# A language model's fused layers: the dense tiles take three PSUM score banks in the order 0, 1, 2, 1

## The chip, the cores and the metric

The kernel runs on one core of a Trainium2 chip. Its time is the device time in microseconds (us); three runs of the kernel before gave 3267.7, 3269.15 and 3270.88 us, and the median is 3269.15 us. The core has five engines that run side by side, each in the order of its own instructions: PE (TensorE, matrix products), ACT (ScalarE), DVE (VectorE), POOL (GpSimd) and SP (which issues transfers). They wait for each other through semaphores. PSUM is the memory that PE writes to; it has eight banks of 128 x 512 f32, and this kernel uses all eight.

## The reference

The reference is a small language model of two layers on 4 sequences of 1024 tokens with 64 channels. The part that matters here is the feed-forward block of the first layer: product keys choose 16 of 4096 values for each token and head, and the values are mixed by a softmax.

```
q = (x @ Wq_pk).reshape(b, n, P, HEADS, DIM_KEY)            # two halves of a query
sim = einsum('pbnhd,pkhd->pbnhk', q, pk_keys)               # 64 scores for each half
scores, idx = top_k(sim, 16)
score = scores[0][..., :, None] + scores[1][..., None, :]   # sums of a row's and a column's score
final_scores, pk_idx = top_k(score, 16)
final_scores = softmax(final_scores)
k = einsum('bnhk,bnhkd->bnhd', final_scores, keys_table[ind])
v = einsum('bnhk,bnhkd->bnhd', final_scores, values_table[ind])
```

The keys and values so found go through causal attention with 8 heads, after that come a plain attention and a mixture of 8 experts. There are 16 (sequence, head of 0 to 3) pairs, and each pair carries a second head (4 to 7) with it.

## The kernel before, in words

A first part (embedding, a convolution by Fourier matrices, a gate) ends in this profile at 353 us. The stage `mixer_stage` follows, and what is said from here on is all in it. It has 22 time slots of 64 positions each (`SLOT = 64`). Every engine has its own loop over all positions `q`, and does at each position what the tables (`area_uses`, `extra_uses`, `STEPS_AT`) put there. So the order on each engine is written out in advance, and the same position of different engines belongs together only through semaphores.

One head of a pair finds its values by gathers of table rows: POOL issues them (L1402), ACT scales the rows (L1691), DVE sums them once in eight positions (L2013). The other head does without gathers, by a dense product over all 4096 values. This dense product is what the change touches. For a pair it has 64 tiles: two halves of 512 tokens, 32 tiles each (`TILES`), each tile 128 values by 512 tokens. In the dense loop `c` numbers the tiles over all pairs, 1024 in all. A tile goes through four steps:

- `score_dense(c)` on PE: the 128 x 512 scores into a PSUM bank `D_ps` (L1417, L1420). The score of a value is a sum of a row's and a column's part. A *corner* is the set of tiles that share the same two operands `U[.., 2 + jh, ..]` and `U[.., ih, ..]`. Within a corner there are eight tiles (`eighth` 0 to 7), and the scores of the next differ from those of the one before by one product. So the bank keeps the scores of the last tile, and one product of 96 x 128 by 96 x 512 in bf16 (L1420) adds the difference. Only where a bank begins a corner, or is taken over in its midst, is a product with `start=True` made first (L1417), and the tile is called *fresh*.
- `exp_dense(c)` on ACT (L1623): the exponential of the bank into `W`, a ring of six buffers in SBUF.
- `mask_dense(c)` on DVE (L1787): reads the bank again and sets to zero in `W` what lies below the threshold. It raises the semaphore `w_done`.
- `apply_dense(c)` on PE (L1430): the product of the table's tile with `W`, summed into `acc`. In the profile it is two instructions, as every f32 product here.

At position `q`, with `c = q - 64`, PE does in this order: the scores of tile `c + 3`, `apply_dense(c)`, the weighting of the attention (`weigh`, L1442), the attention's scores into two other banks called `area` (L1456, L1476, L1486 and more), and one further small task through the bank `X` (L1523 to L1581). ACT does at the same position the exponential of tile `c + 3` and then the rest of its work, DVE its maxima of `area` first, its other work, and the mask of tile `c + 3` among or behind it.

Before the change tile `c` uses bank `c % 3`. Its scores may be written when the mask of tile `c - 3` is done (`pe.wait_ge(w_done, c - 2)`). Since `apply_dense(c)` waits for the mask of tile `c` anyway, that wait and the wait of the scores of tile `c + 3` are for the same mask.

Tiles are named in what follows by their number within the pair, 0 to 63; the first half is 0 to 31, the second 32 to 63. Tile `t` is scored at position `t - 3`. In the order before, the corners of a half are begun at its tiles 0, 1, 2 (one in each bank), and the fourth corner is shared by the three banks at tiles 24, 25, 26 of the half: six fresh tiles in a half.

## Time and profile before

| what | value |
|---|---|
| median of three runs | 3269.15 us |
| span of the profiled execution | 3918.3 us |
| PE busy | 3008.9 us, 77% |
| DVE busy | 2785.8 us, 71% |
| POOL busy | 2057.7 us, 53% |
| ACT busy | 2039.4 us, 52% |
| scores of the dense tiles, L1420 and L1417 | 1024 and 192 matmuls |
| masks of the dense tiles, L1787 | 1024, 683 ns each |

The profiled execution has no time of its own beside its span, so the span stands for it. It is 649.2 us longer than the median of the runs. The busy time of an engine is the union of its instructions; a matmul's end is modelled, and the spacing of the starts of two matmuls that follow each other is shorter than the duration shown.

### The profile page before, as it was taken

The page shows a single profiled execution, that of the slowest core. Times are in us where ns is not written, and L with a number is a line of the kernel's source. Part 1 is how long each engine was busy: PE and PEld are TensorE (multiplying, and loading weights), DVE is VectorE, ACT ScalarE, POOL GpSimd, SP SyncE. Part 2 cuts the span into 40 slices and gives each one's busy share as a digit, 9 for nine tenths or more (in the row PEclk, how much of TensorE's full clock was granted, in tenths as well). Part 3 has the DMA queues.
Part 4 walks back from the last instruction along what each step waited for, and adds up shares of the span by engine and source line. Part 5 has one row for each costly group of instructions (what it writes and reads, how often), then busy time and mean ns, then how long its engine had stood idle before and what let it go on. Part 6 is the DMA issues. An engine that isn't in the chain of part 4 may idle for free.

```text
span 3918.3 us, 39268 instructions
## 1 busy us (share of the span) xinstructions
PE 3008.9 (77%) x9722; PEld 1391.1 (36%) x9722; DVE 2785.8 (71%) x9999; ACT 2039.4 (52%) x4498; POOL 2057.7 (53%) x2095
## 2 busy tenths in 40 slices
PE   4861657878787878878778868888778878888888
PEld 2430223333333333333333433333333433333343
DVE  7678777777777777776777887777768786874433
ACT  3231545555555555655555655556555655555532
POOL 3011666666656665555565655556656655655400
PEclk8985777888787888989888989888888988989899
DMA  1001121212121111112121212111111212121100
GB/s 37 22 8 52 44 66 43 62 45 57 48 56 47 52 52 50 52 46 55 44 59 38 65 40 57 44 52 53 51 50 46 57 46 56 42 62 39 33 3 3
DMA packets 85626, 179.86 MB, mean 46 GB/s; under 512 B 40177, under 2 KB 41107, under 8 KB 85398
## 3 DMA queue, kind: packets, MB, share of 16 engines
q0 software_dynamic: 66560, 135.40, 13.1%
q1 hardware_dynamic: 18838, 41.94, 3.5%
q8 instruction: 79, 1.29, 0.1%
q14 instruction: 149, 1.22, 0.1%
HBM read 176.15 MB, written 1.05 MB: 45 GB/s over the span
## 4 chain that ended last, share of the span: by engine, by line
PE 41%; DVE 25%; another core or an unknown queue 11%; issue 8%; ACT 8%; ACTq 0%; DVEq 0%
PE mx_acc L1430 12%; PE mx_O L1442 7%; PE mx_area L1476 6%; DVE mx_W L1787 5%; PE mx_D L1420 4%; ACT mx_GT L1691 3%; DVE mx_KVs L2013 3%; PE mx_area L1456 2%; ACT mx_W L1623 2%; DVE mx_mx_part L2031 2%; PE mx_area L1492 1%; DVE mx_mx L2031 1%; PE mx_X L1560 1%; PE mx_area L1486 1%
## 5 line engine op out<-in xcount | busy, mean ns | idle before, releaser
L1402 POOL DMA_INDIRECT mx_G<-in_kv_table,mx_slot_i x2048 | 2004.0, 978 | 1394.6 <-issue 590.1
L1430 PE MATMUL mx_acc<-mx_W,mx_table 128*128 128x512 f32 x2048 | 1180.7, 660 | 1.6 <-ACT mx_kvT L1630 0.7
L1787 DVE SCALAR_TENSOR_TENSOR mx_W<-mx_D,mx_W 128x512 f32<-128x512 f32 x1024 | 699.1, 683 | 297.5 <-ACT mx_W L1623 180.5
L1623 ACT ACTIVATE mx_W<-mx_D 128x512 f32<-128x512 f32 x1024 | 606.6, 593 | 523.2 <-PE mx_D L1420 231.0
L1691 ACT ACTIVATE mx_GT<-mx_G,mx_slot_w 128x128 f32<-128x128 f32 x2048 | 759.2, 495 | 3.2 <-DVE mx_KVs L2013 1.1
L1420 PE MATMUL mx_D<-mx_U,mx_pick_b 96*128 96x512 bf16 x1024 | 432.7, 423 | 110.8 <-DVE mx_W L1787 52.5
L1430 PEld LDWEIGHTS mx_acc<-mx_W,mx_table 128*128 128x128 f32 x2048 | 436.1, 214 | 201.9 <-issue 104.5
L1647 ACT ACTIVATE mx_PT<-mx_area 128x512 f32<-128x512 f32 x472 | 241.8, 514 | 464.9 <-PE mx_area L1480 146.3
L1442 PE MATMUL mx_O<-mx_PT,mx_KVs 128*65 128x512 f32 (+3 forms) x768 | 347.5, 536 | 170.0 <-ACT mx_PT L1647 82.8
L1456 PE MATMUL mx_area<-mx_KTa,mx_QTa 64*128 64x512 f32 (+3 forms) x384 | 200.6, 607 | 132.6 <-DVE mx_mx L2031 66.1
L2013 DVE TENSOR_REDUCE mx_KVs<-mx_GT 128x128 f32<-128x2048 f32 x128 | 291.9, 2280 | 6.0 <-ACT mx_GT L1691 5.9
L1442 PEld LDWEIGHTS mx_O<-mx_PT,mx_KVs 128*65 128x65 f32 x768 | 105.4, 146 | 388.3 <-issue 277.5
L1476 PE MATMUL mx_area<-mx_QTa,mx_KTa 65*128 65x512 f32 (+3 forms) x384 | 187.9, 574 | 70.5 <-DVE mx_mx_part L2031 61.3
L1420 PEld LDWEIGHTS mx_D<-mx_U,mx_pick_b 96*128 96x128 bf16 x1024 | 110.2, 108 | 355.7 <-issue 173.2
L1476 PE MATMUL mx_area<-mx_QTb,mx_KTb 128*128 128x512 f32 (+3 forms) x384 | 175.9, 542 | 44.4 <-DVE mx_mx_part L2031 25.6
L1456 PE MATMUL mx_area<-mx_KTb,mx_QTb 64*128 64x512 f32 (+3 forms) x384 | 202.8, 612 | 0.0
L2031 DVE TENSOR_REDUCE mx_mx_part<-mx_area 128x2 f32<-128x1024 f32 (+3 forms) x128 | 130.7, 1021 | 90.5 <-remote 43.0
L2054 DVE RECIPROCAL mx_rz<-mx_X 128x4 f32<-128x4 f32 x72 | 13.0, 180 | 247.1 <-remote 135.2
L1456 PEld LDWEIGHTS mx_area<-mx_KTa,mx_QTa 64*128 64x128 f32 x384 | 64.4, 210 | 291.0 <-issue 172.2
L1476 PEld LDWEIGHTS mx_area<-mx_QTa,mx_KTa 65*128 65x128 f32 x384 | 77.9, 211 | 175.6 <-issue 85.1
L1476 PEld LDWEIGHTS mx_area<-mx_QTb,mx_KTb 128*128 128x128 f32 x384 | 78.1, 209 | 138.9 <-issue 88.7
L1535 PE MATMUL mx_X<-mx_ident_b,mx_PC 128*96 128x128 bf16 x512 | 51.8, 260 | 95.3 <-remote 46.0
(390 smaller groups left out, 4462.4 us busy)
## 6 DMA issues: line engine op xcount, KB each, us to landing
mx_table<-in_kv_dense SPq DMA_DIRECT2D x64, 512.0 KB
mx_G<-in_kv_table,mx_slot_i POOLq DMA_INDIRECT x2048
tz_table<-in_c_dft SPq DMA_DIRECT2D x1, 2048.0 KB
tz_table<-in_c_idft SPq DMA_DIRECT2D x8, 256.0 KB, 2.6
out_h<-mx_xc SPq DMA_DIRECT2D x4, 256.0 KB
mx_G<-in_c_pick SPq DMA_DIRECT2D x1, 528.0 KB
st_h<-in_tok_W,em_ids POOLq DMA_INDIRECT x32
st_keys<-in_pk_keys SPq DMA_DIRECT2D x1, 512.0 KB, 3.9
```

The source lines that it names most:

```text
L1402: pool.indirect_dma_start(G[g % RING][:, r, :], None, a["kv_table"], bass.IndirectOffsetOnAxis(slot_i[n % 2][:, k, r:r + 1], 0))\
L1420: pe.matmul(D_ps[c % 3][:, :], pick_b[:, step, :], U[n % 2][:, ih, cols], start=False, stop=True, skip_group_check=True).then_inc(d_ready, 1)
L1430: pe.matmul(acc[:, :], table[:, tile, :], W[c % TILE_RING][:, :], start=(tile == 0), stop=(tile == TILES - 1)).then_inc(applied, 1)
L1442: pe.matmul(O_ps[0:D + 1, first:HALF], values, PT[k % 4][:, first:HALF], start=(kb == 0), stop=last, skip_group_check=True).then_inc(weigh ...
L1456: last = pe.matmul(area[x][:, 0:w], QT[x][lanes[x], qb * P:qb * P + P], KT[x][lanes[x], kh * HALF:kh * HALF + w], start=True, stop=not dia ...
L1476: last = pe.matmul(bank[:, first:HALF], KT[x][:, kb * P:kb * P + P], QT[x][:, group * HALF + first:(group + 1) * HALF], start=True, stop=n ...
L1623: act.activation(W[c % TILE_RING][:, :], D_ps[c % 3][:, :], ACT.Exp).then_inc(p_done, 1)
L1647: act.activation(PT[k % 4][:, first:HALF], area[cnt.bank[use]][:, first:HALF], ACT.Gelu if use[0] == "HID" else ACT.Exp).then_inc(prob_rea ...
L1691: last = act.activation(GT[:, :, i], G[g % RING][:, i, :], ACT.Copy, scale=slot_w[n % 2][:, k, i:i + 1])
L1787: dve.scalar_tensor_tensor(W[c % TILE_RING][:, :], D_ps[c % 3][:, :], 0.0, W[c % TILE_RING][:, :], ALU.is_ge, ALU.mult).then_inc(w_done, 1)
L2013: dve.tensor_reduce(both, rows, AX, ALU.add).then_inc(kv_ready, 1)
L2031: dve.tensor_reduce(dst, banks[:, :, 0:w], AX, ALU.max).then_inc(scores_taken, 2)
```

## The change

Tiles take the banks in the order 0, 1, 2, 1 (`BANK_OF`, by `c % 4`). Odd tiles all use bank 1, even tiles banks 0 and 2 in turn. A half has 16 odd tiles in bank 1, which are two corners of eight, and 8 tiles each in banks 0 and 2, which are one corner each. So the corners begin at the tiles 0, 1, 2 and 17 of a half, and nowhere else: four fresh tiles and not six. `corner_of` says which corner and eighth a tile is; the table of values is laid out by the same function, outside the kernel, so its tiles come in the new order by themselves. The wait before the scores follows the bank: an even tile waits for the mask of tile `c - 4`, an odd one for the mask of tile `c - 2`.

```
 RING = 2
 TILE_RING = 6
+BANK_OF = (0, 1, 2, 1)
...
 def corner_of(tile):
-    bank, step = tile % 3, tile // 3
-    pair, eighth = (bank, step) if step < 8 else (3, 3 * bank + step - 8)
-    return pair // 2, pair % 2, eighth, step in (0, 8)
+    if tile % 2:
+        pair, eighth = 2 + tile // 16, tile // 2 % 8
+    else:
+        pair, eighth = tile // 2 % 2, tile // 4
+    return pair // 2, pair % 2, eighth, eighth == 0
...
+        def D_of(c):
+            return D_ps[BANK_OF[c % 4]][:, :]
...
                 if c >= 3:
-                    pe.wait_ge(w_done, c - 2)
+                    pe.wait_ge(w_done, c - 1 if c % 2 else c - 3)
                 if fresh:
-                    pe.matmul(D_ps[c % 3][:, :], pick_b[:, 0, :], U[n % 2][:, 2 + jh, cols], start=True, stop=False,
+                    pe.matmul(D_of(c), pick_b[:, 0, :], U[n % 2][:, 2 + jh, cols], start=True, stop=False,
                               skip_group_check=True)
-                step = 1 + eighth // 3 if fresh else 3 + eighth
-                pe.matmul(D_ps[c % 3][:, :], pick_b[:, step, :], U[n % 2][:, ih, cols],
+                step = 1 if fresh else 3 + eighth
+                pe.matmul(D_of(c), pick_b[:, step, :], U[n % 2][:, ih, cols],
                           start=False, stop=True, skip_group_check=True).then_inc(d_ready, 1)
...
-                act.activation(W[c % TILE_RING][:, :], D_ps[c % 3][:, :], ACT.Exp).then_inc(p_done, 1)
+                act.activation(W[c % TILE_RING][:, :], D_of(c), ACT.Exp).then_inc(p_done, 1)
...
-                dve.scalar_tensor_tensor(W[c % TILE_RING][:, :], D_ps[c % 3][:, :], 0.0, W[c % TILE_RING][:, :],
+                dve.scalar_tensor_tensor(W[c % TILE_RING][:, :], D_of(c), 0.0, W[c % TILE_RING][:, :],
                                          ALU.is_ge, ALU.mult).then_inc(w_done, 1)
```

The change touches the order of PE alone; ACT, DVE, POOL and SP keep every instruction in its place. `mx_D0` to `mx_D2` are the three banks, `mx_W0` to `mx_W5` the ring, `mx_U0` the operand of the first pair; the lines of the changed kernel are numbered six higher, L1423 for L1417, L1426 for L1420, L1436 for L1430. The first place is PE in the second half of the first pair, at the scores of tiles 56, 57 and 58, before:

```order
L1417 MATMUL mx_D2<-mx_U0,mx_pick_b 128x512 [waits mx_w_done]
L1420 MATMUL mx_D2<-mx_U0,mx_pick_b 128x512
L1430 MATMUL mx_acc<-mx_W5,mx_table 128x512 [waits mx_w_done]
L1417 MATMUL mx_D0<-mx_U0,mx_pick_b 128x512 [waits mx_w_done]
L1420 MATMUL mx_D0<-mx_U0,mx_pick_b 128x512
L1430 MATMUL mx_acc<-mx_W0,mx_table 128x512 [waits mx_w_done]
L1417 MATMUL mx_D1<-mx_U0,mx_pick_b 128x512 [waits mx_w_done]
L1420 MATMUL mx_D1<-mx_U0,mx_pick_b 128x512
L1430 MATMUL mx_acc<-mx_W1,mx_table 128x512 [waits mx_w_done]
```

The same three tiles on PE now:

```order
L1426 MATMUL mx_D0<-mx_U0,mx_pick_b 128x512 [waits mx_w_done]
L1436 MATMUL mx_acc<-mx_W5,mx_table 128x512 [waits mx_w_done]
L1426 MATMUL mx_D1<-mx_U0,mx_pick_b 128x512 [waits mx_w_done]
L1436 MATMUL mx_acc<-mx_W0,mx_table 128x512 [waits mx_w_done]
L1426 MATMUL mx_D2<-mx_U0,mx_pick_b 128x512 [waits mx_w_done]
L1436 MATMUL mx_acc<-mx_W1,mx_table 128x512 [waits mx_w_done]
```

Three matmuls are gone here, and the banks stand in another order. The second place is PE in the same half at the scores of tiles 48, 49 and 50, before:

```order
L1420 MATMUL mx_D0<-mx_U0,mx_pick_b 128x512 [waits mx_w_done]
L1430 MATMUL mx_acc<-mx_W3,mx_table 128x512 [waits mx_w_done]
L1420 MATMUL mx_D1<-mx_U0,mx_pick_b 128x512 [waits mx_w_done]
L1430 MATMUL mx_acc<-mx_W4,mx_table 128x512 [waits mx_w_done]
L1420 MATMUL mx_D2<-mx_U0,mx_pick_b 128x512 [waits mx_w_done]
L1430 MATMUL mx_acc<-mx_W5,mx_table 128x512 [waits mx_w_done]
```

Tiles 47 to 50 on PE now, the first two rows being tile 47 and what follows it:

```order
L1426 MATMUL mx_D1<-mx_U0,mx_pick_b 128x512 [waits mx_w_done]
L1436 MATMUL mx_acc<-mx_W2,mx_table 128x512 [waits mx_w_done]
L1426 MATMUL mx_D0<-mx_U0,mx_pick_b 128x512 [waits mx_w_done]
L1436 MATMUL mx_acc<-mx_W3,mx_table 128x512 [waits mx_w_done]
L1423 MATMUL mx_D1<-mx_U0,mx_pick_b 128x512 [waits mx_w_done]
L1426 MATMUL mx_D1<-mx_U0,mx_pick_b 128x512
L1436 MATMUL mx_acc<-mx_W4,mx_table 128x512 [waits mx_w_done]
L1426 MATMUL mx_D2<-mx_U0,mx_pick_b 128x512 [waits mx_w_done]
L1436 MATMUL mx_acc<-mx_W5,mx_table 128x512 [waits mx_w_done]
```

Tile 49 is tile 17 of the second half and is fresh now, so one matmul is added; it goes to bank `mx_D1`, which tile 47 used two tiles earlier.

## Rows read from the trace of the kernel before

**Rows 1.** The profile's page: span, then busy time and share of each engine.

```profile
span 3918.3 us, 39268 instructions
PE 3008.9 (77%) x9722; PEld 1391.1 (36%) x9722; DVE 2785.8 (71%) x9999; ACT 2039.4 (52%) x4498; POOL 2057.7 (53%) x2095
```

**Rows 2.** The page's chain of waits, share of the span by engine.

```profile
PE 41%; DVE 25%; another core or an unknown queue 11%; issue 8%; ACT 8%; ACTq 0%; DVEq 0%
```

**Rows 3.** Busy time by stretch: us, PE, PEld, DVE, ACT, POOL busy (count), PEclk, DMA.

```profile
353.00:3711.00 3358.00, 2628.79 (x8360) 1189.00 (x8361) 2448.72 (x9099) 1871.63 (x4196) 2000.40 (x2045) 0.86 0.18 50
...
1551.00:1560.00 9.00, 9.00 (x21) 3.90 (x22) 5.85 (x35) 5.33 (x13) 6.54 (x7) 0.64 0.33 97
1560.00:1576.00 16.00, 16.00 (x53) 7.52 (x52) 12.96 (x72) 8.90 (x22) 11.00 (x13) 1.00 0.18 48
```

**Rows 4.** Instructions on mx_D: ns min/median/max, first and last start.

```profile
L1417 PE MATMUL mx_D<-mx_U,mx_pick_b x192: 379/381/634, 353.4 to 3690.9; 96*128 96x512 bf16 x192
```

**Rows 5.** The chain of waits in order of time, second halves: start, us, what.

```profile
747.36 0.22 PE mx_D L1417
...
1570.46 0.22 PE mx_D L1417
1570.68 0.22 PE mx_D L1420
...
3691.04 0.22 PE mx_D L1417
```

**Rows 6.** The chain of waits by line, 1645 to 1652 us, first half of pair 6.

```profile
by line: DVE mx_V L1814 29.8%; DVE mx_mxl_part L2042 25.6%; issue 24.0%; DVE mx_W L1787 17.0%; DVE mx_S L1808 11.1%; DVE mx_I L1807 5.5%
```

**Rows 7.** Timeline, tiles 13 to 15 of pair 6: start, us, instruction, idle before it.

```profile
1646.14 0.38 PE L1420 MATMUL mx_D<-mx_U,mx_pick_b 96*128 96x512 bf16 x1
...
1646.20 0.68 DVE L1787 SCALAR_TENSOR_TENSOR mx_W<-mx_D,mx_W 128x512 f32<-128x512 f32 x1
...
1646.56 0.60 ACT L1623 ACTIVATE mx_W<-mx_D 128x512 f32<-128x512 f32 x1 [0.70 <-issue]
...
1649.62 2.07 PE L1486 MATMUL mx_area<-mx_KTl,mx_QTl 128*128 128x512 f32 x2 [2.24 <-remote]
...
1652.70 0.67 DVE L1787 SCALAR_TENSOR_TENSOR mx_W<-mx_D,mx_W 128x512 f32<-128x512 f32 x1
```

**Rows 8.** Timeline, mask of tile 43 and scores of tile 45, pair 5.

```profile
1533.50 0.68 DVE L1787 SCALAR_TENSOR_TENSOR mx_W<-mx_D,mx_W 128x512 f32<-128x512 f32 x1
...
1534.18 0.38 PE L1420 MATMUL mx_D<-mx_U,mx_pick_b 96*128 96x512 bf16 x1
```

**Rows 9.** Timeline, masks of tiles 46 and 47 and scores of tile 49, pair 5.

```profile
1539.95 0.67 DVE L1787 SCALAR_TENSOR_TENSOR mx_W<-mx_D,mx_W 128x512 f32<-128x512 f32 x1
...
1542.20 1.02 PE L1476 MATMUL mx_area<-mx_QTa,mx_KTa 65*128 65x512 f32 x2
...
1544.09 0.39 PE L1420 MATMUL mx_D<-mx_U,mx_pick_b 96*128 96x512 bf16 x1 [0.87 <-remote]
...
1548.37 0.18 DVE L2054 RECIPROCAL mx_rz<-mx_X 128x4 f32<-128x4 f32 x1 [7.75 <-remote]
...
1550.23 0.68 DVE L1787 SCALAR_TENSOR_TENSOR mx_W<-mx_D,mx_W 128x512 f32<-128x512 f32 x1
```

**Rows 10.** Timeline, a mask and the scores that waited for it.

```profile
490.65 0.68 DVE L1787 SCALAR_TENSOR_TENSOR mx_W<-mx_D,mx_W 128x512 f32<-128x512 f32 x1
...
491.39 0.39 PE L1420 MATMUL mx_D<-mx_U,mx_pick_b 96*128 96x512 bf16 x1 [0.91 <-DVE mx_W L1787]
```

**Rows 11.** Timeline, first and last odd tile scored ahead of the mask two tiles back.

```profile
401.01 0.39 PE L1420 MATMUL mx_D<-mx_U,mx_pick_b 96*128 96x512 bf16 x1 [0.29 <-DVE mx_W L1787]
401.89 0.67 DVE L1787 SCALAR_TENSOR_TENSOR mx_W<-mx_D,mx_W 128x512 f32<-128x512 f32 x1
...
3692.11 0.69 DVE L1787 SCALAR_TENSOR_TENSOR mx_W<-mx_D,mx_W 128x512 f32<-128x512 f32 x1 [3.43 <-issue]
3692.39 0.38 PE L1420 MATMUL mx_D<-mx_U,mx_pick_b 96*128 96x512 bf16 x1
```

## The prediction

> **What bounds the kernel now.** I read the page first. PE is busy 77% of the span and DVE 71% [rows 1], and the chain that ended last gives PE 41%, DVE 25%, and 11% to something the profile can't name [rows 2]. So neither engine alone sets the time. The busy time by stretch says the same: in the mixer, from 353 to 3711 us, PE is busy 2628.8 of 3358 us and DVE 2448.7 [rows 3]. Only a look at where in a pair each of them leads helps.
>
> The chain in order of time, laid against the tile numbers, gives a clear pattern. In the second half of a pair it runs along PE: from 1560 to 1576 us PE is busy all 16 us at a granted clock of 1.00 [rows 3], and the products for fresh tiles stand one behind the other in the chain, 0.22 us each [rows 5]. In the first half, from about tile 15 to 38, it runs along DVE: between 1645 and 1652 us every named line of it is DVE's [rows 6]. This matters, since the change takes matmuls from PE and tightens PE's wait for DVE.
>
> The profiled span is 3918.3 us [rows 1], 649.2 us above the median of 3269.15 us. Much of that is stalls of the profiled execution: at 1540 us DVE stands 7.75 us until something the profile can't name [rows 9], and the same gap comes back at the same tile of most pairs. I take them as absent from the timed runs, an assumption the traces can't prove. The sum is therefore a difference in us of durations at full clock, made on the profiled execution and carried over to the median unscaled.
>
> **The change part by part.** *Matmuls removed.* 32 halves had six fresh tiles, 192 in all [rows 4]; now they have four. Removed are 32 x 3 = 96 products at tiles 24 to 26 of a half, added are 32 at its tile 17: 64 fewer. The duration shown is 381 ns [rows 4], but a matmul that follows another starts 0.22 us after it [rows 5], and this is what one costs PE. All 64 are 64 x 0.22 = 14.1 us of PE's time.
>
> The Trainium skill, Perfetto Trace Analysis, section "Tensor Engine Instruction (MATMUL, LD_WEIGHTS)", says that the profiler estimates a matmul's end from its size and does not observe it. By the duration the 64 would be worth 24.4 us, by the spacing 14.1 us; the trace sides with the spacing.
>
> What of them lies on the path? In the chain of waits I counted the products of the old fresh tiles. Of the 48 in second halves (tiles 56 to 58) 38 are on it, the first at 747.36 and the last at 3691.04 us [rows 5]; of the 48 in first halves (tiles 24 to 26) 4. Removing them gives 42 x 0.22 = 9.2 us. The added ones: in the second half tile 49 lies in the stretch that PE leads, so all 16 count, 16 x 0.22 = 3.5 us. In the first half tile 17 lies where the chain passes to DVE; I take 8 of 16, 1.8 us. Net gain: 9.2 - 3.5 - 1.8 = 3.9 us. The ends are 0 and 14.1 us.
>
> *The wait of odd tiles.* It was for the mask three tiles back, it is now for the mask two back. Behind it on PE, in order, stand the apply of tile c - 3, the attention's weighting and scores, and the small task in bank X; ACT waits for all of them. In the trace of before, 157 of the 508 odd tiles from the ninth on were scored before the mask two back had ended, the first by 1.55 us (401.89 + 0.67 - 401.01) and the last by 0.41 us [rows 11]. Over all of them this is 296 us of PE held back. This is the largest number of the case, and nearly all of it should cost nothing:
>
> It happens where DVE is behind, and there PE's work isn't wanted yet. Tile 15 of pair 6 was scored at 1646.14, while the mask of tile 13 ended at 1646.88 us; it would be held 0.74 us and 0.06 for the semaphore. But PE stands 2.24 us at the next scores for L1486 anyway, which need DVE too, and the mask of tile 15 starts only at 1652.70, 5.5 us after the exponential's end at 1647.16 [rows 7]. The delay is gone before anybody misses it. Where the attention's scores are consumed by DVE, at positions 16 to 38 and the early ones of the plain attention, PE can't run two positions ahead in any case.
>
> What is left are the second halves, which PE leads. The mask of tile 43 ends at 1534.18, and tile 45 is scored at 1534.18 us [rows 8]. It would be held by the semaphore alone; a matmul that waited started 0.06 us after the mask's end (490.65 + 0.68 to 491.39) [rows 10]. 16 x 0.06 = 1.0 us. Tile 49 was scored at 1544.09, after an idle time that the stall made; PE was free at 1542.20 + 0.86 = 1543.06 (two f32 matmuls, by their spacing). The mask of tile 47 needs, from DVE's reciprocal to its own end, 1550.91 - 1548.37 = 2.54 us, and could have begun at 1540.62, so it would end at 1543.16 [rows 9]. Hold: 0.10 + 0.06 = 0.16 us, in 16 pairs 2.6 us. Tile 59 looks worse in the profile, but its exponential had been held by a stall too. So the wait costs 3.6 us. The ends: 0, if PE soon stands for the attention's output anyway and that swallows it, and 296 us, which would need every hold to reach the end; the row nearest to the second halves is tile 49's, and I stay with it.
>
> *The wait of even tiles.* It is for the mask four back, so the scores no longer stand for the mask that the apply behind them needs. After such a wait PE has 0.22 us less to do. Where PE waits for a mask DVE leads, so I take 0; the other end is 16 such places on PE's stretches, -3.5 us.
>
> *The bank itself.* Exponential and mask keep their form and their order, and each bank still has one writer and two readers in turn. 0. The first part and the last 207 us of the span contain none of these lines: 0.
>
> **Sum.** -3.9 + 3.6 + 0 = -0.3 us. Predicted: 3269.15 - 0.3 = 3269 us, no change within what a measurement can tell. A difference of 0.2% (6.5 us) is about what a measurement of this kernel can tell from none.
>
> **Rivals.** *Faster: the second halves take the whole gain.* PE is busy 16 of 16 us there [rows 3], and all three of the removed products are on the chain. If the holds at tiles 45 and 49 vanish in PE's idle time behind them, if the 16 added at tile 49 lie beside a wait as well, and if even tiles give back their 3.5 us, the gain is 9.2 + 3.5 = 12.7 us: 3256 us. For it: the three stand in a stretch without one gap. Against it: part of that stretch is the backlog of the stall before it, which the timed runs don't have, and then DVE, with 12.96 of 16 us busy, may lead there now and then. Chance 0.29.
>
> *Slower: the odd tile's wait costs a position of lead behind each heavy mask.* DVE's sum over the gathered rows stands ahead of the masks of tiles 3, 11, 19 and so on, which are all odd, so it is always the tile two later, odd too, that stands for it. PE then comes to its work of that position late, and with a stock of two positions instead of three DVE runs dry when its light positions follow. It decides from the point at which DVE, once past the heavy mask, is quicker through a position than PE. Price: without tiles 49 and 59 the holds sum to 187 us; the part of them at tiles 1 to 15 and 39 to 63, outside the positions where DVE's maxima hold PE anyway, is 73 us. If a third of that reaches the end it is 24 us, and with the 3.6 us above and without 3.9 gained it is 3269.15 + 28 = 3297 us; a sixth gives 3285. Against it: PE at these places was ahead by as much as it would be held. Chance 0.24 for everything above 3276 by this way.
>
> *Slower: the clock.* After the stall that ends at 1548 us [rows 9] its granted clock is 0.64 on average for 9 us, where it is 1.00 afterwards [rows 3]: the lower level of 1.2 GHz for the larger part of it. If longer stands brought one more such fall in each pair, PE would lose 0.36 x 9 = 3.2 us each time, 52 us in all: 3321 us. The holds found are below 2 us nearly everywhere, so I give it 0.04.
>
> The Trainium skill, TensorE: Matmul & The Clock Gate, section "A second HAM failure mode: psum-queue depth-cycling", says that short idles between groups of matmuls while cycling through PSUM banks can make the clock swing. Here the banks cycle before and after alike. It would be the case just named; by the page alone it could be likely, by the rows it is not.
>
> *The change does less than it says.* The order of PE shows 64 matmuls fewer, so this is excluded.
>
> **How the numbers follow.** No change 0.43 (3263 to 3276 us), faster 0.29, slower by the lost lead 0.24, slower by the clock 0.04. That makes faster by over 0.2% 0.29, within 0.2% 0.43, slower 0.28. The range leaves out a little of each end: from 3254, the whole gain, to 3290, where a fifth of the 73 us and a little more would reach the end. The likeliest case alone is 3263 to 3276 us.
>
> **What would show it.** In the changed kernel's profile L1423 must stand 128 times. If the sum is right, the waits of PE for masks move from even to odd tiles and grow in total, while DVE's idle time ahead of its masks stays. If the faster rival holds, the chain in second halves has lost the three products and gained nothing at tiles 45 and 49. If the slower one holds, DVE idles more before the masks of tiles 4 to 8 and 46 to 50, behind ACT, which waits for PE. The prediction is wrong if the median is outside 3263 to 3276 us, and its sum is wrong, even with the median right, if DVE's idle time ahead of its masks moves by more than a third.

## The result, and the profile after

The change made the kernel a little slower. Seven runs of the changed kernel have a median of 3280.16 us (3275.51 to 3285.37), seven runs of the kernel before beside them 3270.88 us (3266.13 to 3274.51). The ratio is 1.0027, with a 95% interval of 1.0014 to 1.0040. The prediction was 3269 us and no change; the measured 0.27% is small, but its interval leaves out zero. The median lies outside the 3263 to 3276 us that the prediction had named for its likeliest case. Three executions in the whole case took far longer (4128.66, 7041.87 and 15431.88 us), and the ratios leave them out.

The page of the changed kernel, span, busy time and chain of waits, answers to [rows 1, 2]:

```profile
span 3273.6 us, 39140 instructions
PE 2786.8 (85%) x9658; PEld 1315.2 (40%) x9658; DVE 2749.4 (84%) x9999; ACT 2021.9 (62%) x4498; POOL 2061.7 (63%) x2095
...
PE 39%; DVE 28%; POOL 10%; issue 7%; ACT 5%; DMA 2%; POOLq 0%; ACTq 0%; DVEq 0%
```

Two things are new. The span is 645 us shorter than the 3918.3 us of [rows 1], and lies where the timed runs lie. And POOL, which no step of the prediction spoke of, has a tenth of the chain. Neither is the change's doing. The kernel before, profiled once more as the run `e0_before`, gives nearly the same page:

```profile
span 3274.6 us, 39268 instructions
PE 2793.2 (85%) x9722; PEld 1324.8 (40%) x9722; DVE 2748.5 (84%) x9999; ACT 2018.2 (62%) x4498; POOL 2058.3 (63%) x2095
...
PE 39%; DVE 30%; POOL 9%; issue 6%; ACT 5%; DMA 2%; ACTq 0%; DVEq 0%; POOLq 0%
...
L1402 POOL DMA_INDIRECT mx_G<-in_kv_table,mx_slot_i x2048 | 2002.3, 978 | 776.3 <-issue 605.1
...
L1691 ACT ACTIVATE mx_GT<-mx_G,mx_slot_w 128x128 f32<-128x128 f32 x2048 | 759.4, 494 | 218.9 <-DMA mx_G<-in_kv_table,mx_slot_i 217.5
L1787 DVE SCALAR_TENSOR_TENSOR mx_W<-mx_D,mx_W 128x512 f32<-128x512 f32 x1024 | 696.8, 681 | 208.4 <-ACT mx_W L1623 205.9
L1623 ACT ACTIVATE mx_W<-mx_D 128x512 f32<-128x512 f32 x1024 | 605.3, 592 | 191.7 <-PE mx_D L1420 188.6
...
L1420 PE MATMUL mx_D<-mx_U,mx_pick_b 96*128 96x512 bf16 x1024 | 407.7, 398 | 56.8 <-DVE mx_W L1787 56.1
```

So the "unknown" 11% of [rows 2] and the stalls of [rows 9] belonged to that one profiled execution. The comparisons below are made against `e0_before`. The same groups of the changed kernel, by the columns instructions | busy us, mean ns | idle us of the engine just before them, and what ended it:

```profile
L1408 POOL DMA_INDIRECT mx_G<-in_kv_table,mx_slot_i x2048 | 2003.3, 978 | 779.0 <-issue 608.2
...
L1793 DVE SCALAR_TENSOR_TENSOR mx_W<-mx_D,mx_W 128x512 f32<-128x512 f32 x1024 | 699.5, 683 | 208.9 <-ACT mx_W L1629 206.7
L1629 ACT ACTIVATE mx_W<-mx_D 128x512 f32<-128x512 f32 x1024 | 605.4, 592 | 252.1 <-PE mx_D L1426 249.0
L1426 PE MATMUL mx_D<-mx_U,mx_pick_b 96*128 96x512 bf16 x1024 | 410.1, 400 | 154.0 <-DVE mx_W L1793 153.1
```

PE now stands 154.0 us ahead of the scores, nearly all of it for masks, where it stood 56.8. That is 97 us more; ACT's idle time ahead of the exponentials grows by 60 (191.7 to 252.1). In the sum of DVE's idle time ahead of the masks almost nothing arrives (208.4 to 208.9). The last number is what the prediction had asked for, and it holds, while the timed runs are 9 us slower. The two profiled executions differ by 1 us only; that of `e0_before` was the slowest of its kernel's 12 runs (3276.48 us against a median of 3266.01). One execution scatters by as much as is sought here, so a sum over one profile can't decide a question of 0.3%; only what stands tile by tile, and the same in several kernels, can.

The products are as announced, one line of the changed kernel's instructions on L1423:

```profile
L1423 PE MATMUL mx_D<-mx_U,mx_pick_b x128: 378/381/634, 338.9 to 3030.8; 96*128 96x512 bf16 x128
```

### The profile page after: what moved, and what is told of

It reads as the page before. It is cut to its first block, busy times and chain, and to the rows that moved or that the text cites. A ratio compares the mean times of both kernels' runs of the same rounds, so it can differ in the third digit from the quotient of the medians.

```text
span 3273.6 us, 39140 instructions
## 1 busy us (share of the span) xinstructions
PE 2786.8 (85%) x9658; PEld 1315.2 (40%) x9658; DVE 2749.4 (84%) x9999; ACT 2021.9 (62%) x4498; POOL 2061.7 (63%) x2095
## 3 DMA queue, kind: packets, MB, share of 16 engines
q8 instruction: 78, 1.28, 0.2%
## 4 chain that ended last, share of the span: by engine, by line
PE 39%; DVE 28%; POOL 10%; issue 7%; ACT 5%; DMA 2%; POOLq 0%; ACTq 0%; DVEq 0%
PE mx_acc L1436 12%; POOL mx_G L1408 10%; PE mx_O L1448 6%; DVE mx_W L1793 6%; PE mx_area L1482 6%; PE mx_D L1426 3%; DVE mx_KVs L2019 3%; DMA mx_G<-in_kv_table,mx_slot_i 2%; DVE mx_mx_part L2037 2%; PE mx_area L1462 2%; ACT mx_GT L1697 2%; PE mx_area L1498 2%; PE mx_X L1566 1%; ACT mx_W L1629 1%; DVE mx_mx L2037 1%
## 5 line engine op out<-in xcount | busy, mean ns | idle before, releaser
L1436 PE MATMUL mx_acc<-mx_W,mx_table 128*128 128x512 f32 x2048 | 1108.0, 623 | 0.0
L1793 DVE SCALAR_TENSOR_TENSOR mx_W<-mx_D,mx_W 128x512 f32<-128x512 f32 x1024 | 699.5, 683 | 208.9 <-ACT mx_W L1629 206.7
L1629 ACT ACTIVATE mx_W<-mx_D 128x512 f32<-128x512 f32 x1024 | 605.4, 592 | 252.1 <-PE mx_D L1426 249.0
L1426 PE MATMUL mx_D<-mx_U,mx_pick_b 96*128 96x512 bf16 x1024 | 410.1, 400 | 154.0 <-DVE mx_W L1793 153.1
L1436 PEld LDWEIGHTS mx_acc<-mx_W,mx_table 128*128 128x128 f32 x2048 | 410.3, 202 | 164.1 <-issue 99.4
L1448 PE MATMUL mx_O<-mx_PT,mx_KVs 128*65 128x512 f32 (+3 forms) x768 | 311.9, 488 | 14.7 <-ACT mx_PT L1653 13.8
L1426 PEld LDWEIGHTS mx_D<-mx_U,mx_pick_b 96*128 96x128 bf16 x1024 | 106.0, 103 | 393.4 <-DVE mx_W L1793 271.2
L1482 PE MATMUL mx_area<-mx_QTa,mx_KTa 65*128 65x512 f32 (+3 forms) x384 | 171.5, 529 | 58.2 <-DVE mx_mx_part L2037 58.2
L1462 PE MATMUL mx_area<-mx_KTb,mx_QTb 64*128 64x512 f32 (+3 forms) x384 | 195.3, 592 | 0.0
L1482 PE MATMUL mx_area<-mx_QTb,mx_KTb 128*128 128x512 f32 (+3 forms) x384 | 157.6, 492 | 9.3 <-DVE mx_mx_part L2037 9.3
L1533 PE MATMUL mx_X<-st_keys,mx_qpk 128*128 128x256 f32 x256 | 77.3, 429 | 52.7 <-ACT mx_S L1665 32.4
L1710 ACT ACTIVATE mx_hot<-mx_FI 128x864 uint16<-128x864 uint32 x128 | 116.4, 911 | 3.6 <-DVE mx_row L1972 3.6
```

The source lines that it names most:

```text
L1426: pe.matmul(D_of(c), pick_b[:, step, :], U[n % 2][:, ih, cols], start=False, stop=True, skip_group_check=True).then_inc(d_ready, 1)
L1436: pe.matmul(acc[:, :], table[:, tile, :], W[c % TILE_RING][:, :], start=(tile == 0), stop=(tile == TILES - 1)).then_inc(applied, 1)
L1448: pe.matmul(O_ps[0:D + 1, first:HALF], values, PT[k % 4][:, first:HALF], start=(kb == 0), stop=last, skip_group_check=True).then_inc(weigh ...
L1462: last = pe.matmul(area[x][:, 0:w], QT[x][lanes[x], qb * P:qb * P + P], KT[x][lanes[x], kh * HALF:kh * HALF + w], start=True, stop=not dia ...
L1482: last = pe.matmul(bank[:, first:HALF], KT[x][:, kb * P:kb * P + P], QT[x][:, group * HALF + first:(group + 1) * HALF], start=True, stop=n ...
L1629: act.activation(W[c % TILE_RING][:, :], D_of(c), ACT.Exp).then_inc(p_done, 1)
```

## The experiments

Every kernel was timed in five rounds against the kernel before; the ratio stands with its 95% interval. Pairs are counted from 0. "Period" is the time from the end of one tile's mask to the end of the next, and sums of periods are over the pairs 1 to 15.

### The change in two: its wait and its products

`e0_before` is the kernel before, unchanged, for a second profile and as a measure of what no change looks like.

> The kernel before, unchanged, for a profile of its own beside the others. The profiled execution shown ahead of the prediction stood 649 us above its timed runs; both theories expect that this one comes out near 3272 us with a span of about the same, as the changed kernel's did (3273.6 us), and that it shows where ACT and DVE really stand. Time 3271 us.

Measured: 0.9992 (0.9980 to 1.0003), 3266.01 us.

`e1_wait_alone` is the kernel before with the odd tiles' wait of the change:

```
-                    pe.wait_ge(w_done, c - 2)
+                    pe.wait_ge(w_done, c - 1 if c % 2 else c - 2)
```

> Banks, corners and products of the kernel before; only the wait of odd tiles is tightened, from the mask three tiles back to the mask two back. Theory A (the lost lead of the odd tiles makes the change slow, and hides a gain of some 4 us of the removed products): slower than before by 9 to 14 us, about 3283 us. Theory B (the wait costs nothing, and the loss comes from the other parts, the earlier scores of even tiles or the new banks): within 3 us of before, 3271 us.

Measured: 1.0024 (1.0011 to 1.0037), 3276.1 us. The wait alone is, within the intervals, the whole slowdown.

`e2_products_alone` is the kernel before with the change's number and places of fresh products; its banks are the old ones, so the scores after tile 16 of a half are other than the reference's:

```
-    return pair // 2, pair % 2, eighth, step in (0, 8)
+    return pair // 2, pair % 2, eighth, tile in (0, 1, 2, 17)
```

> Banks and waits of the kernel before; the products that begin a bank stand at tiles 0, 1, 2 and 17 of a half, as in the change, and no longer at 24, 25, 26. The scores after tile 16 of a half are wrong by this, the work is the changed kernel's. Theory A: 4 us faster than before (3267), at most 14. Theory B: no change or up to 4 us faster as well; it is the difference of this run and the changed kernel that they must both explain.

Measured: 1.0003 (0.9992 to 1.0014), 3268.3 us. By the interval the 64 products fewer are worth between 2.6 us of gain and 4.6 us of loss. The two parts, 1.0024 and 1.0003, make up the 1.0027 of the change.

`e3_other_parity` lets the even tiles take the short wait. The heavy masks, those behind DVE's sum over gathered rows, are of tiles 3, 11, 19 and so on; an even tile never waits directly for one of them.

```
-BANK_OF = (0, 1, 2, 1)
+BANK_OF = (1, 0, 1, 2)
...
-    if tile % 2:
+    if tile % 2 == 0:
...
-                if c >= 3:
-                    pe.wait_ge(w_done, c - 1 if c % 2 else c - 3)
+                if c >= 4 or c == 2:
+                    pe.wait_ge(w_done, c - 3 if c % 2 else c - 1)
```

> The changed kernel with the parts of even and odd swapped: even tiles all use bank 1, odd tiles banks 0 and 2. The long sum of gathered rows on DVE stands ahead of odd tiles' masks, so the tile held by the mask two back is no longer the one that follows a heavy mask. Fresh tiles are 0, 1, 3 and 16 of a half. Theory A, in its form that the heavy mask is what holds: most of the loss is gone, 3265 to 3270 us. If any wait two back costs the same, whatever the parity: as the changed kernel, 3280 us. Theory B: 3280 us too, or unlike both.

Measured: 1.0035 (1.0024 to 1.0046), 3279.67 us. My theory that it takes a heavy mask fell: without one in the short wait it is no better. A lead of two tiles costs as much at the even tiles as at the odd ones.

### Banks, even tiles, and where the wait costs

`e4_banks_six_products` is the changed kernel with six products in a half, so that only banks and waits differ from before; without a fresh product at tile 17 and with those at the tiles 24 to 26 the scores from tile 17 on are other than the reference's.

```
-    return pair // 2, pair % 2, eighth, eighth == 0
+    return pair // 2, pair % 2, eighth, tile in (0, 1, 2, 24, 25, 26)
```

> The changed kernel's banks and waits, but with the beginning products at tiles 0, 1, 2, 24, 25 and 26 of a half as before, 192 in all (the scores of tiles 17 on are wrong by this, the work is that of six products). Theory A, as the first four runs leave it (the odd tiles' wait is the loss of some 8 us, the products are worth nothing): 3276 to 3280 us, as the changed kernel. If the products had been worth 4 us beside the new waits: 3284.

Measured: 1.0031 (1.0019 to 1.0043), 3277.19 us: as the change itself. `e5_even_as_before` takes from the change the looser wait of its even tiles:

```
-                    pe.wait_ge(w_done, c - 1 if c % 2 else c - 3)
+                    pe.wait_ge(w_done, c - 1 if c % 2 else c - 2)
```

> The changed kernel, with the wait of even tiles for the mask three tiles back, as before, in place of four back. Theory A: no difference to the changed kernel (3276 to 3280), since an even tile's apply waits for that mask anyway. Theory C (the earlier scores of even tiles disturb ACT's order and cost): faster than the changed kernel by 2 us or more.

Measured: 1.0022 (1.0013 to 1.0031), 3275.88 us. The looser wait of the even tiles brings nothing, as predicted.

`e6_wait_tiles_11_to_31` and `e11_wait_other_tiles` (this one ran in the next group) divide the short wait by place: odd tiles 11 to 31 of a pair, and all other odd tiles.

```
-                    pe.wait_ge(w_done, c - 2)
+                    pe.wait_ge(w_done, c - 1 if c % 2 and 11 <= c % SLOT < 32 else c - 2)
```

> The kernel before with the odd wait tightened at tiles 11 to 31 of a pair only, the place where the profile shows nearly all of PE's added idle time (0.4 to 1.2 us a tile) and DVE's added idle time ahead of the masks of tiles 14 and 15 (0.32 us a pair together). If the loss arises there: 5 to 8 us slower than before, as the tightening everywhere. If it arises at tile 5 and in the second half: within 2 us of before.

> The kernel before with the odd wait tightened at the tiles 0 to 10 and 32 to 63 of a pair, that is everywhere but at 11 to 31. With the run of tiles 11 to 31 (3276 us by its ratio of 1.002) it divides the loss of 8 us. If the loss is made at tiles 14 and 15, as DVE's added idle time there says: within 2 us of before. If tile 5 and the second half carry a part, as I first reckoned: 3 to 4 us slower.

Measured: 1.0020 (1.0007 to 1.0032) for the tiles 11 to 31, 1.0011 (1.0001 to 1.0022) for the others. By these values eleven of 32 odd tiles carry about two thirds, and they lie in the stretch in which I had judged the wait free; the two intervals overlap over most of their length, so the share itself is not shown, only that each part costs something.

`e7_apply_first` is the changed kernel with PE's apply of a position ahead of the odd tile's scores. If the loss came from the apply and the attention that stand behind a held matmul, this would have given it back.

```
-                if 0 <= c + 3 < PAIRS * SLOT:
+                if 0 <= c + 3 < PAIRS * SLOT and not (c % 2 == 0 and c >= 0 and c % TILES):
...
+                    if c % 2 == 0 and c + 3 < PAIRS * SLOT:
+                        score_dense(c + 3)
```

> The changed kernel, with the scores of an odd tile put behind apply_dense of the same position and not ahead of it (not at the first tile of a half). While PE waits for the mask two back it then has the apply, 0.86 us, to do. Theory A (the wait blocks what stands behind it): 3 to 8 us faster than the changed kernel, about 3272. If what counts is that the scores themselves come late, ACT and DVE behind them: slower than the changed kernel, 3285 or more.

Measured: 1.0065 (1.0050 to 1.0080), 3289.72 us. The theory fell, and in a useful way: the order that frees the apply and makes the scores still later costs more. It is the scores that are wanted, by ACT: against the changed kernel PE stands less ahead of the scores (154.0 to 86.1 us), but ACT's idle time ahead of the exponentials grows from 252.1 to 354.1 us and DVE's ahead of the masks from 208.9 to 259.0.

### The gathers as a floor

POOL's part of the chain asked for a test of its own. In the kernel before 2048 gathers are issued from 332.7 to 3057.4 us, 1.33 us apart on average. Where nothing holds them they are mostly 1.25 us apart, 0.94 busy and 0.30 that the profile names "issue"; the second of these two lines is one of the longer ones:

```profile
1000.00 0.94 POOL L1402 DMA_INDIRECT mx_G<-in_kv_table,mx_slot_i  x1 [0.30 <-issue]
1001.24 1.19 POOL L1402 DMA_INDIRECT mx_G<-in_kv_table,mx_slot_i  x1 [0.30 <-issue]
```

That is 128 x 1.25 = 160 us in a pair. From the last mask of one pair to that of the next it takes 162 to 171 us in eleven pairs and 177 to 180 in the other four. In the profile shown of before nobody could see it: the stalls gave POOL time to run ahead, and ACT hardly ever stood for a gather. The two groups of that page:

```profile
L1402 POOL DMA_INDIRECT mx_G<-in_kv_table,mx_slot_i x2048 | 2004.0, 978 | 1394.6 <-issue 590.1
...
L1691 ACT ACTIVATE mx_GT<-mx_G,mx_slot_w 128x128 f32<-128x128 f32 x2048 | 759.2, 495 | 3.2 <-DVE mx_KVs L2013 1.1
```

ACT's idle time ahead of the scaling is 3.2 us here and 218.9 us in `e0_before`. `e8_fifteen_rows` leaves out the gather of the sixteenth row from the third group on; the old content of the buffer is used in its place.

```
-                for r in range(TOPK):
+                for r in range(TOPK if g < RING else TOPK - 1):
...
-                    act.wait_ge(gathered[g % RING], 16 * TOPK * (g // RING + 1))
+                    act.wait_ge(gathered[g % RING], 16 * (TOPK + (TOPK - 1) * (g // RING)))
```

> The kernel before, with POOL issuing the gathers of 15 table rows and not 16 for every group after the first two (the sixteenth row of a group keeps an old value; 126 gathers left out). Theory D (POOL's row of gathers, 2048 issues 1.25 us apart, is a floor under the mixer: 2560 of the 2724 us from its first to its last): much faster, by 60 to 150 us, until DVE or PE holds. If POOL is only one of several and off the path: within 15 us of before.

Measured: 0.9789 (0.9775 to 0.9802), 3197.8 us. One gather in sixteen gone takes 70 us off, and ACT's idle time ahead of the scaling falls to 80.6 us. The floor is real. On this ground, where the other engines set the pace more often, the two parts were tried again: `e9_fifteen_rows_products` with the products of `e2_products_alone`, `e10_fifteen_rows_wait` with the wait of `e1_wait_alone`.

> As the last, with the beginning products at tiles 0, 1, 2, 17 of a half too (64 fewer). Theory D: the 64 products, worth nothing while the gathers set the pace, are worth 4 to 10 us here against the fifteen rows alone. If the gathers have nothing to do with it: within 2 us of the fifteen rows alone.

> As the fifteen rows alone, with the odd tiles' wait tightened to the mask two back. If the wait delays the chain PE, ACT, DVE itself: 8 us or more slower than the fifteen rows alone. If it only works through the gathers, which wait for masks and for ACT's scaling: within 3 us.

Measured: 0.9797 (0.9784 to 0.9811), 3201.22 us, for the products, which is no gain and so neither of the two expectations; 0.9814 (0.9801 to 0.9827), 3207.75 us, for the wait, 10 us slower than `e8_fifteen_rows`, and the runs of the two don't overlap (3197.44 to 3203.52 against 3206.63 to 3208.92). So the wait's cost isn't bound to the gathers: it is as large where their floor is loosened.

`e12_rows_three_fresh` takes away all three products at tiles 24 to 26 of a half and adds none, 96 fewer; the scores from tile 24 on are other than the reference's.

```
-    return pair // 2, pair % 2, eighth, step in (0, 8)
+    return pair // 2, pair % 2, eighth, tile in (0, 1, 2)
```

> Fifteen rows as before, and the beginning products at tiles 0, 1, 2 of a half only: 96 fewer, none added at tile 17. The profiles of fifteen rows with and without the change of products give, as means over 15 pairs, 0.40 us a pair less between the masks of tiles 55 and 60 and 0.18 us more at the mask of tile 50, behind the product added at tile 49. If both are real: 3.5 us less for the removed and added ones together, which two timed runs didn't show, and 6.4 us less here than fifteen rows alone, 3191 to 3194 us. If the removed ones are hidden after all: 3197 to 3200 us.

Measured: 0.9810 (0.9794 to 0.9825), 3204.24 us, where a real gain would have given some 3192. Its expectation was missed.

`e13_rows_wait_13_15` is `e8_fifteen_rows` with the short wait at two tiles of a pair alone:

```
-                    pe.wait_ge(w_done, c - 2)
+                    pe.wait_ge(w_done, c - 1 if c % SLOT in (13, 15) else c - 2)
```

> Fifteen rows as before, and the odd wait tightened at the tiles 13 and 15 of a pair only, 32 of 1024 tiles. The profile of fifteen rows with all odd waits tightened has 0.15 us a pair more at the mask of tile 15 and 0.30 us more at tile 17. If these two waits are the main part of the loss of 10 us: 5 to 8 us slower than fifteen rows alone, 3203 to 3206. If it is spread over all odd tiles: within 2 us of it.

Measured: 0.9815 (0.9801 to 0.9828), 3206.14 us. By the medians these 32 waits of 512 carry 8 of the 10 us. The comparison is a loose one: the two kernels were not timed in the same group, and `e12_rows_three_fresh`, which was timed beside this one and has no short wait, came out at 3204.24 us, 2 us below it. What can be compared tile by tile is firmer, and this is the run in which the mechanism can be read. First the timeline of pair 3 in `e8_fifteen_rows`: scores of 13, mask of 11, scores, exponential of 15, mask of 13, exponential and mask of 17 (start, us, instruction, idle before it and its releaser):

```profile
857.76 0.38 PE L1420 MATMUL mx_D<-mx_U,mx_pick_b 96*128 96x512 bf16 x1
857.96 0.68 DVE L1787 SCALAR_TENSOR_TENSOR mx_W<-mx_D,mx_W 128x512 f32<-128x512 f32 x1
...
860.93 0.39 PE L1420 MATMUL mx_D<-mx_U,mx_pick_b 96*128 96x512 bf16 x1 [0.85 <-DVE mx_W L1787]
861.36 0.60 ACT L1623 ACTIVATE mx_W<-mx_D 128x512 f32<-128x512 f32 x1 [0.20 <-PE mx_D L1420]
...
861.95 0.68 DVE L1787 SCALAR_TENSOR_TENSOR mx_W<-mx_D,mx_W 128x512 f32<-128x512 f32 x1
...
866.62 0.60 ACT L1623 ACTIVATE mx_W<-mx_D 128x512 f32<-128x512 f32 x1
...
867.92 0.67 DVE L1787 SCALAR_TENSOR_TENSOR mx_W<-mx_D,mx_W 128x512 f32<-128x512 f32 x1
```

The same pair in `e13_rows_wait_13_15`: mask of 11, scores of 13, mask of 13, scores and exponential of 15, exponential and mask of 17:

```profile
853.94 0.68 DVE L1787 SCALAR_TENSOR_TENSOR mx_W<-mx_D,mx_W 128x512 f32<-128x512 f32 x1
854.68 0.39 PE L1420 MATMUL mx_D<-mx_U,mx_pick_b 96*128 96x512 bf16 x1 [0.93 <-DVE mx_W L1787]
...
857.93 0.68 DVE L1787 SCALAR_TENSOR_TENSOR mx_W<-mx_D,mx_W 128x512 f32<-128x512 f32 x1
858.67 0.39 PE L1420 MATMUL mx_D<-mx_U,mx_pick_b 96*128 96x512 bf16 x1 [1.66 <-DVE mx_W L1787]
859.10 0.60 ACT L1623 ACTIVATE mx_W<-mx_D 128x512 f32<-128x512 f32 x1 [1.01 <-PE mx_D L1420]
...
864.35 0.60 ACT L1623 ACTIVATE mx_W<-mx_D 128x512 f32<-128x512 f32 x1
...
864.98 0.69 DVE L1787 SCALAR_TENSOR_TENSOR mx_W<-mx_D,mx_W 128x512 f32<-128x512 f32 x1 [1.00 <-ACT mx_W L1623]
```

Count from the start of mask 13. Its end holds the scores of 15, so they come at +0.74 where they came at -1.02. The exponential of 15 comes at +1.17 where it came at -0.59. From there to the exponential of 17 ACT has 5.25 us of work without a gap in both (exponentials, scaling, two copies of keys for each position), so that one comes at +6.42 where it came at +4.67. Mask 17 had started 0.70 us after that exponential's end, which is all that DVE had in hand; now it stands 1.00 us, and mask 17 starts at +7.05, before at +5.97. Of the 1.76 us nearly 0.7 are absorbed and 1.08 paid, not where the hold is but two tiles later. In pairs 2, 3, 4 and 5 the period of tile 17 is longer by 1.1 us each, in pairs 9 and 13 that of tile 15 by 1.0 each, 6.4 us together; `e10_fifteen_rows_wait` has the same to 0.2 us, and tile 5 of pairs 9 and 13 longer by 1.0 each besides. The other ten pairs show nothing at these tiles.

Two limits belong to this reading. The loss at tile 17 exists on fifteen rows only: with all sixteen, in `e0_before`, the mask of tile 17 already stands 1.15 us in pair 3, and its period is 2.62 us there and 2.63 in the changed kernel. And in pairs 9 and 13 of this run the granted clock fell to 0.66 for 5 us behind the held scores of tile 13, so these two are not the hold alone; the part on the clock comes back to this.

### The pace of the gathers

POOL's gathers are throttled by a wait for a mask some positions back. `e14_before_pace_10` lets them run four positions further ahead in the kernel before, `e15_after_pace_10` does the same in the changed one:

```
-                    ahead = SLOT * n + 8 * k - 6 + r // 2
+                    ahead = SLOT * n + 8 * k - 10 + r // 2
```

> The kernel before, with POOL's wait for masks loosened by four tiles (its gathers may run up to 10 tiles ahead and not 6). POOL waits 92 us for masks in the profile of before. Theory D (the gathers are the floor, and each wait of POOL before a light stretch comes back as a late gather): 10 to 60 us faster. If its waits for masks only stand in for waits for ACT's scaling, which frees the ring of two: no change.

> The changed kernel with the same loosened pace of POOL. Theory A alone: as much slower than the kernel before with the same pace as now, 8 us. With the gathers no longer the floor the removed products may show and bring it to 4 us.

Measured: 0.9979 (0.9969 to 0.9988), 3261.18 us, for the kernel before, and 1.0013 (1.0004 to 1.0022), 3271.49 us, for the changed one. The first beats both kernels of this case, by 5 us by the medians and 7 by the ratio, less than the 10 to 60 expected. The change costs 10.3 us on this ground too, not 4. POOL's wait for masks goes down from 92.3 us in `e0_before` to 38.4 us, this line of the waits of `e14_before_pace_10`, while its wait for ACT's scaling goes up from 26.0 to 61.5 us:

```profile
POOL mx_G L1402 <- DVE mx_W L1787: 38.4, 115, 3.6
```

### What a product is worth on each side

The last two runs ask why products that stood on the chain brought nothing. The kernel before repeats each of the three fresh products at tiles 24 to 26 of a half, so that it is made four times: in the second halves in `e16_products_second_half`, in the first in `e17_products_first_half` (`half == 0`). It is 144 matmuls more each, 31.7 us of PE.

```
-                if fresh:
+                for _ in range(4 if fresh and tile >= 24 and half == 1 else fresh):
```

> The kernel before, with the beginning product of tiles 56, 57 and 58 of a pair made four times in place of once: 144 more matmuls, 31.7 us of PE's time at 0.22 us. If a product there lies on the path, as the chain of waits said of 38 in 48: 20 to 32 us slower. If it is hidden or its time comes back from a later wait: within 8 us of before.

> The same at tiles 24, 25 and 26 of a pair, the fresh tiles of the first half: 144 more matmuls, 31.7 us. The chain of waits had 4 of 48 there on the path, and DVE is behind PE there: within 4 us of before. If PE's lead over DVE counts there: 10 us slower or more.

Measured: 1.0036 (1.0023 to 1.0050), 3281.24 us, in the second halves: about 12 us, 0.08 us for a product, between the two expectations. In the first halves 1.0004 (0.9993 to 1.0015), 3270.37 us: nothing. My reading of who leads where, PE at tiles 56 to 58 and DVE at 24 to 26, is supported by this pair. But a product on PE's stretch is worth 0.08 us and not 0.22. The periods of `e16_products_second_half` say where the rest stays: the tiles 56 to 58 are longer by 7.9 + 2.4 + 16.0 = 26.3 us over 15 pairs, 0.19 us for each of their 135 products, which is nearly the full price. Tile 62 gives back 7.9 us: there ACT waits for gathers, 32.6 us over these pairs in `e0_before` and 10.9 here, so a later arrival waits less. Tiles 0, 6 and 22 are shorter by 4.5, 5.9 and 7.2 us, but tile 22 is shorter by 6.1 us in `e14_before_pace_10` as well, without one product more, so that these belong to the products is not shown.

## Why the prediction was wrong

**What bounds the kernel.** The alternation of PE and DVE was read rightly [rows 3, 5, 6]; the pair of runs above shows it. What was missed is the third party. The page said POOL 53%, and I passed over it. A queue whose instructions are 0.94 us long and 1.25 us apart is full at 75% busy, and the stalls of the profiled execution had hidden the rest. This omission isn't what made the forecast miss, since the wait costs as much on fifteen rows, where that floor is loosened.

**Products.** The forecast was -3.9 us; alone they measured between -2.6 and +4.6. Place and size of the parts were nearly right: in `e2_products_alone` the tiles 56, 58 and 60 are shorter by 6.3 us in 15 pairs (forecast 38 x 0.22 = 8.4 in 16), tile 50 is longer by 2.2 us (forecast 3.5). But tile 62 is longer by 5.5 us, where kernels with the products of before are longer by 0.4 to 3.3. It is the term's passage from the chain to the end that was mis-sized: at 0.08 us for a product on PE's stretch the 48 removed and 16 added there come to 32 x 0.08 = 2.6 us of gain, which the runs can't tell from none.

**The wait of odd tiles: the step that failed.** The prediction put the holds in first halves at nothing. It read "It happens where DVE is behind, and there PE's work isn't wanted yet", and took tile 15 of pair 6 as its witness [rows 7]. The witness was right for its pair: in pair 6 nothing is lost at tile 15 in the changed kernel. It was wrong for the step. The check looked at DVE (the mask starts long after the exponential) and at PE (it soon waits anyway), and not at ACT, which stands between them with a sequence of its own. Where that sequence is nearly as full as DVE's, a held score shifts the whole of it, and DVE meets the delay tiles later. In the changed kernel itself a part of it is seen in pair 13. First `e0_before`: scores 13, mask 11, exponential 13, scores 15, mask 13, ACT's load of a function table, exponential and mask of 15:

```profile
2592.28 0.38 PE L1420 MATMUL mx_D<-mx_U,mx_pick_b 96*128 96x512 bf16 x1
...
2593.65 0.68 DVE L1787 SCALAR_TENSOR_TENSOR mx_W<-mx_D,mx_W 128x512 f32<-128x512 f32 x1
...
2594.38 0.60 ACT L1623 ACTIVATE mx_W<-mx_D 128x512 f32<-128x512 f32 x1
...
2597.19 0.38 PE L1420 MATMUL mx_D<-mx_U,mx_pick_b 96*128 96x512 bf16 x1
...
2597.64 0.68 DVE L1787 SCALAR_TENSOR_TENSOR mx_W<-mx_D,mx_W 128x512 f32<-128x512 f32 x1
...
2599.76 1.28 ACT L1623 ACT_TABLE_LOAD   x1
...
2601.06 0.60 ACT L1623 ACTIVATE mx_W<-mx_D 128x512 f32<-128x512 f32 x1
...
2601.68 0.69 DVE L1787 SCALAR_TENSOR_TENSOR mx_W<-mx_D,mx_W 128x512 f32<-128x512 f32 x1 [0.74 <-ACT mx_W L1623]
```

Then the changed kernel: mask 11, scores 13, exponentials 13 and 14, mask 13, scores 15, table load, exponential and mask of 15:

```profile
2596.23 0.68 DVE L1793 SCALAR_TENSOR_TENSOR mx_W<-mx_D,mx_W 128x512 f32<-128x512 f32 x1
2596.97 0.39 PE L1426 MATMUL mx_D<-mx_U,mx_pick_b 96*128 96x512 bf16 x1 [1.95 <-DVE mx_W L1793]
2597.40 0.60 ACT L1629 ACTIVATE mx_W<-mx_D 128x512 f32<-128x512 f32 x1 [0.44 <-PE mx_D L1426]
...
2599.14 0.60 ACT L1629 ACTIVATE mx_W<-mx_D 128x512 f32<-128x512 f32 x1 [0.17 <-PE mx_D L1426]
...
2600.22 0.68 DVE L1793 SCALAR_TENSOR_TENSOR mx_W<-mx_D,mx_W 128x512 f32<-128x512 f32 x1
...
2602.54 0.38 PE L1426 MATMUL mx_D<-mx_U,mx_pick_b 96*128 96x512 bf16 x1
...
2603.35 1.28 ACT L1629 ACT_TABLE_LOAD   x1
...
2604.65 0.60 ACT L1629 ACTIVATE mx_W<-mx_D 128x512 f32<-128x512 f32 x1
...
2605.28 0.69 DVE L1793 SCALAR_TENSOR_TENSOR mx_W<-mx_D,mx_W 128x512 f32<-128x512 f32 x1 [1.75 <-ACT mx_W L1629]
```

The scores of 13 move from 1.37 us ahead of the start of mask 11 to 0.74 us behind it, and from mask 11 to mask 15 it is 9.05 us where it was 8.03. ACT has no gap ahead of the exponential of 15 in either. What makes its sequence so full in this pair is that it changes between two functions and loads a table of 1.28 us at each change, two of them between the exponentials of 14 and 15. It waits 0.44 us for the held scores of 13, which is less than half of the 1.02 us; the rest comes where PE runs at the lower clock behind the hold.

The periods of this kind that the changed kernel and `e1_wait_alone` have in common are tiles 5 and 15 in pairs 9 and 13, together 3.8 and 4.1 us. They are not a mark of the short wait alone: `e16_products_second_half`, whose waits are those of before, has the same four longer by 4.1 us, and `e14_before_pace_10` and `e17_products_first_half` have one of the four each, by 1.0 and 1.4 us. In all of them PE comes later to these places. With the short wait at all odd tiles all four are longer in every profile; in the other kernels with sixteen rows it varies. So for the changed kernel these tiles fit the mechanism, but their 3.8 us are not shown to be due to the wait, and they are less than half of what the runs measured.

**The numbers of that step.** For the wait 3.6 us were forecast, all of them for tiles 45 and 49. At neither does a period in `e1_wait_alone` differ from `e0_before` by over 0.7 us in 15 pairs, so the loss is not there. The wait's measured cost, 8.6 us (`e1_wait_alone` against the kernel before on the same chip, 3267.55 us), 10.0 us (`e10_fifteen_rows_wait` against `e8_fifteen_rows`) or, with the products, 10.3 us (`e15_after_pace_10` against `e14_before_pace_10`), was within the ends that I had named, 0 and 296 us, but the value was taken from the wrong row. At the odd tiles 21 to 29 PE stands 0.4 to 1.5 us each on average in the changed kernel, up to twice as long as at 13 and 15 (0.8 and 0.7), and this is free as predicted: the periods of these tiles are not longer in `e10_fifteen_rows_wait`.

**The rivals.** "The odd tile's wait costs a position of lead" was the right case, with the right chain: ACT waits for PE, and DVE runs dry when light positions follow a heavy mask. It had 0.24, for everything above 3276 us, and 3280.16 us is above. Its condition was wrong (`e3_other_parity`), its place half (tile 5 is there, tiles 46 to 49 are not, and tile 50 is longer with the added product alone; tile 15 came in their stead, on fifteen rows tile 17 too), and the prices it worked out were too high: 16 us for the smaller one, 9 came.

**The clock.** Another such rival, with 0.04, is there in small. After the hold of 1.95 us in pair 13 PE's granted clock is 0.66 on average for 5 us, of the two levels of 1.2 and 2.4 GHz the lower for most of the time; this row of the changed kernel (stretch, length, busy us of PE, PEld, DVE, ACT, POOL, granted clock):

```profile
2597.50:2602.50 5.00, 5.00 (x9) 1.97 (x8) 5.00 (x35) 4.82 (x10) 3.78 (x5) 0.66 0.20 53
```

In `e0_before` the same tiles, 2592 to 2602 us, run at 1.00. More than half of the loss at tile 15 there comes with it, the 1.02 us less the 0.44 for the held scores: ACT finds the scores of 14, and a result of PE that it takes behind them, late as well. `e10_fifteen_rows_wait` loses 1.1 us at that tile with no such fall, but it is no test of this, since its scores of tile 12, ahead of the hold, already come 1.2 us later against mask 11. Of the 16 pairs of the changed kernel one has the fall between the scores of 13 and 16, so there it is worth about 0.6 us of 9; in pairs 2 to 5 of `e13_rows_wait_13_15`, where tile 17 loses 4.4 us, the clock stays at 1.00. Over the span the clock is 0.926 after and 0.923 before. The Trainium skill, TensorE: Matmul & The Clock Gate, section "A second HAM failure mode: psum-queue depth-cycling", would have the clock swing with short idles between groups; this case's traces agree for single places and not for the kernel.

**Of the signs that the prediction had named** two held and misled: PE's waits for masks grew in total, and DVE's idle time ahead of its masks stayed. The sum of an idle time is no test for a loss of 9 us when one execution differs from the next by as much.

**Still open.** Where most of the 9 us of the change arise. The periods that differ at tiles 5, 15 and 17 come to 6 to 9 us on fifteen rows, where the runs give 8 to 10; with all rows, as in the change itself, they come to 3 to 4 us of 9, and tile 17 has no part in them. That the tiles 13 and 15 carry most of it was tried on fifteen rows only; at the places where gathers are waited for (tiles 6, 7, 14, 22, 62) sums of periods go up and down by up to 8 us from one profile to the next, in kernels with no short wait as well, and I can't assign these. Nor is it shown why in the kernels with fifteen rows the products give 3 to 6 us in the profiles and nothing, or even a loss of 3 to 6 us, in the timed runs.

## What to carry to other kernels

When a wait is made tighter, follow the held result through every engine between it and the one that leads, and ask of each how much time it has in hand over the next several tiles; that the leader isn't waiting at that moment proves nothing. Before a longer period is put down to a change, look at the same place in kernels that don't have it: one found there too isn't its mark. Compute for each queue the spacing of its instructions times their number, the queue that only issues gathers too: it can be a floor at 63% busy, and time saved in front of such a floor comes back behind it. If the profiled span is far above the timed runs, take a second profile before reading who bounds the kernel.

## What the runs showed of the hardware

- Two profiled executions of the same kernel had spans of 3918.3 and 3274.6 us. The longer one had stalls of several us at the same tiles of most pairs, and its idle time ahead of gathered data was 3.2 us where the other showed 218.9.
- Gathers of one row for each of 128 partitions were issued 1.25 us apart, 0.94 of it busy.
- Four positions more of lead for the gathers, a change of one constant, was worth 5 us by the medians and 7 by the ratio (0.9979) where the change of the score banks cost 9.
- A stand of PE of 1.94 to 1.96 us ahead of the scores of tile 13 was followed by 5 us at a granted clock of 0.66 all nine times that it occurs in pairs 9 and 13 of the profiles (the changed kernel, `e1_wait_alone`, `e5_even_as_before`, `e6_wait_tiles_11_to_31`, `e13_rows_wait_13_15`, `e15_after_pace_10`), while the clock stayed at 1.00 through PE's stands of 0.93 and 1.66 us in pair 3 of `e13_rows_wait_13_15`. The length of the stand alone does not decide it: in pair 5 of `e11_wait_other_tiles` the 5 us behind a stand of 0.98 us ran at 0.66 too.
- A change between two functions on ACT took an instruction of 1.28 us (`ACT_TABLE_LOAD`), and in pair 13 two of them stood between the exponentials of tiles 14 and 15.
